# A CIN tower on one core: upper halves of x_pair on ScalarE's queue, alternating PSUM banks, a reordered start

## What is computed

```python
x0 = h = x
for i in range(3):                       # W0: 128 x (32*32), W1 and W2: 128 x (32*64)
    z = (x0[:, :, None, :] * h[:, None, :, :]).reshape(B, F * G, E)
    y = relu(einsum('oc,bce->boe', Ws[i], z) + bs[i][None, :, None])
    if i != n_layers - 1:
        x_keep, h = y[:, :half, :], y[:, half:, :]     # 64 channels are kept, 64 go on
    else:
        x_keep, h = y, y
    xs.append(x_keep)
z = sum(concatenate(xs, axis=1), axis=2)
h = concatenate([z, dense_ctx], axis=1)
h = maximum(h @ W_top1 + b_top1, 0)      # 272 -> 512
h = maximum(h @ W_top2 + b_top2, 0)      # 512 -> 256
y = h @ W_top3                           # 256 -> 1
```

## Time and profile before

| What | Value |
|---|---|
| median of 3 runs | 572.45 us (571.4 to 572.52) |
| the profiled execution: time, span in the profile | 572.41 us, 570.4 us |
| TensorE matmul busy | 526.1 us, 92% |
| VectorE, ScalarE, GpSimd busy | 359.9 us, 135.6 us, 191.6 us |
| direct matmuls (line 559) | 1024 instructions, 451.3 us busy, 31.2 us idle before them |
| DMA over the span | 94.46 MB, mean 166 GB/s |
| mean granted clock of TensorE | 0.976 of full speed |

### The profile page before, as it was taken

The page is one execution under the profiler, slowest core; times in us unless marked ns, Lnnn a source line. Parts: engine busy times, 40 slices in busy tenths (PEclk is TensorE's granted clock), DMA queues, the critical chain, the costliest instruction groups (busy, mean ns, idle before and its releaser), DMA issues.

```text
span 570.4 us, 3875 instructions
## 1 busy us (share of the span) xinstructions
PE 526.1 (92%) x1362; PEld 255.9 (45%) x1362; DVE 359.9 (63%) x212; ACT 135.6 (24%) x193; POOL 191.6 (34%) x162
## 2 busy tenths in 40 slices
PE   2986079699999999999999999999999999999998
PEld 2632034345454544445454545454544445454445
DVE  1243157393949586776949393939495876857642
ACT  1111014312314041414131222213040414130313
POOL 5770072635160707061524334251703030300000
PEclk9988769989999999999999999999999999999999
DMA  6799898279697969697969797796968595540100
GB/s 220 144 187 212 194 263 177 57 201 200 154 230 155 224 146 226 143 230 151 229 141 227 152 239 162 188 214 148 225 149 228 135 236 132 131 94 9 71 0 1
DMA packets 33588, 94.46 MB, mean 166 GB/s; under 512 B 7889, under 2 KB 15057, under 8 KB 25122
## 3 DMA queue, kind: packets, MB, share of 16 engines
q1 hardware_dynamic: 26402, 91.47, 67.3%
q0 software_dynamic: 4096, 1.06, 1.6%
q10 hardware_dynamic: 3072, 1.70, 1.4%
HBM read 92.04 MB, written 2.10 MB: 165 GB/s over the span
## 4 chain that ended last, share of the span: by engine, by line
PE 84%; DMA 8%; POOL 3%; DVE 2%; ACT 1%; issue 1%; ACTq 1%; SPq 0%; DVEq 0%
PE acc L559 74%; PE acc L570 7%; DMA x_rot<-x_scratch 4%; POOL gathered L313 3%; DMA x_scratch<-gathered 2%; DMA gathered<-in_table,rows_all 2%; PE acc L580 1%; DVE z L378 1%; PE acc L575 1%; ACT h L472 0%; DMA row<-in_row 0%; DVE z L366 0%; ACTq L259 0%; PE h L580 0%; ACT kept L472 0%
## 5 line engine op out<-in xcount | busy, mean ns | idle before, releaser
L559 PE MATMUL acc<-z,w_direct 128*128 128x512 f32 x1024 | 451.3, 601 | 31.2 <-DVE z L378 25.7
L559 PEld LDWEIGHTS acc<-z,w_direct 128*128 128x128 f32 x1024 | 196.5, 193 | 276.6 <-issue 243.3
L378 DVE TENSOR_TENSOR z<-h,x_pair 128x2048 f32<-128x2048 f32 (+1 forms) x65 | 144.9, 2250 | 141.3 <-ACT h L472 135.2
L326 POOL TENSOR_TENSOR z_low<-z,z_high 128x1024 fp32r<-128x1024 f32 x30 | 70.2, 2361 | 260.8 <-ACT z_high L458 260.8
L313 POOL DMA_INDIRECT gathered<-in_table,rows_all x128 | 121.1, 946 | 40.7 <-issue 36.0
L378 DVE TENSOR_TENSOR z<-h_odd,x_pair 128x2048 f32<-128x2048 f32 x32 | 72.2, 2279 | 8.8 <-ACT h_odd L472 8.8
L378 DVE TENSOR_TENSOR z<-h_even,x_pair 128x2048 f32<-128x2048 f32 x32 | 72.2, 2279 | 5.2 <-ACT h_even L472 5.2
L472 ACT ACTIVATE h<-acc,columns 64x512 f32<-64x512 f32 x32 | 20.8, 652 | 221.0 <-PE acc L570 215.5
L458 ACT ACTIVATE z_high<-z 128x1024 fp32r<-128x1024 f32 x30 | 30.1, 1049 | 72.4 <-DVE z L366 72.4
L472 ACT ACTIVATE kept<-acc,columns 64x512 f32<-64x512 f32 (+1 forms) x48 | 32.8, 683 | 54.6 <-PE acc L559 53.8
L366 DVE TENSOR_TENSOR z<-x_rep,x_rot 128x2048 f32<-128x2048 f32 x15 | 34.2, 2280 | 16.6 <-DMA x_rot<-x_scratch 16.6
(11 more groups left out here) (119 smaller groups left out, 116.4 us busy)
## 6 DMA issues: line engine op xcount, KB each, us to landing
x_pair<-x_scratch SPq DMA_DIRECT2D x128, 512.0 KB, 6.8
x_rot<-x_scratch SPq DMA_DIRECT2D x56, 256.0 KB, 5.2
x_rep<-x_scratch SPq DMA_DIRECT2D x14, 256.0 KB, 5.0
w_direct<-in_W SPq DMA_DIRECT2D x2, 1024.0 KB, 8.9
gathered<-in_table,rows_all POOLq DMA_INDIRECT x128, 7.1
x_scratch<-gathered SPq DMA_DIRECT2D x30, 64.0 KB, 9.3
x_rot<-x_scratch ACTq DMA_DIRECT2D x4, 256.0 KB, 18.2
x_pair<-in_W_top SPq DMA_DIRECT2D x2, 512.0 KB, 4.3
```

Source lines behind the costliest of these rows:

```text
L326: nc.gpsimd.tensor_tensor(z_low[:, slot_of(pair)], products_of(pair), z_high[:, slot_of(pair)].bitcast(F32), ALU.subtract).then_inc(low_po ...
L378: nc.vector.tensor_tensor(z[:, step.group % Z_SLOTS, first:end], h[:].unsqueeze(1).to_broadcast([P, end - first, N]), x_pair[:, chunk % 2, ...
L559: op = nc.tensor.matmul(acc[pair.layer][:], w_direct[:, first + i], products_of(pair)[:, i], start=i == 0 and pair is OPENS[pair.layer, pa ...
```

## The change

Five things are edited.

1. `load_pair` is split into `load_half`. SyncE's queue issues the lower halves (a = 0) of every chunk, ScalarE's queue the upper halves (a = 1). For chunk 0 and chunk 1 they stand as blocks of four near the head of ScalarE's program, each behind a wait for that chunk's `x_stored`; from chunk 2 on one stands behind each layer-2 step, with a wait for that step's products.
2. `store_x(1)` and `load_x0(1)` go from ScalarE's to SyncE's program, behind chunk 0's lower halves and ahead of chunk 1's.
3. Layers 1 and 2 alternate between two PSUM banks: layer 1 between `spare` (even chunks) and `acc[1]`, layer 2 between `x_bank` and `acc[2]`. `open_bank` waits for the chunk before the last.
4. The places of `layer_out` in ScalarE's program are a table `OUTPUTS`: layer 1 comes ahead of the next chunk's layer 0, layer 2 one step earlier. In `FIRST` the step (0, 2, 0) stands two places earlier in TensorE's order of products, behind (1, 1, 0).
5. The dense input is transposed ahead of TensorE's first transposes (`BUSY` is 56, was 64), and rounded on ScalarE and VectorE there; before, it stood inside chunk 1.

The diff, cut to what matters:

```diff
-BUSY = 64
+BUSY = 56
...
 FIRST = ([(1, 0, k) for k in range(GROUPS)] + [(2, 0, 0), (0, 1, 0)] + [(2, 0, k) for k in range(1, GROUPS)]
-         + [(1, 1, 0), (1, 1, 1), (0, 2, 0), (1, 1, 2), (1, 1, 3)])
+         + [(1, 1, 0), (0, 2, 0)] + [(1, 1, k) for k in range(1, GROUPS)])
...
+def outputs():
+
+    at = {(0, c): PLACE[1, c, 0] for c in range(CHUNKS)}
+    at |= {(1, c): PLACE[2, c - 1, GROUPS - 1] if c >= 2 else PLACE[2, c, 0] for c in range(CHUNKS)}
+    at |= {(2, c): PLACE[2, c + 1, 0] if c else PLACE[1, 1, 1] for c in range(CHUNKS - 1)}
+    return at
...
+        banks = [[acc[0], acc[0]], [spare, acc[1]], [x_bank, acc[2]]]
...
+        def load_half(eng, c, k, a):
+            rows = x_dram[c, ROT * a + GROUP * k:ROT * a + GROUP * (k + 1), :]
+            eng.dma_start(x_pair[HALF * a:HALF * (a + 1), c % 2, GROUP * k:GROUP * (k + 1), :],
+                          rows.unsqueeze(0).to_broadcast([HALF, GROUP, N])).then_inc(xp_here[c % 2][k], 16)
...
             store_x(sp, 0)
-            for c in range(2):
-                for k in range(GROUPS):
-                    load_pair(c, k)
+            sp.wait_ge(x_stored[0], 32)
+            for k in range(GROUPS):
+                load_half(sp, 0, k, 0)
+            store_x(sp, 1)
+            sp.wait_ge(start_done, 1)
+            load_x0(sp, 1)
+            for k in range(GROUPS):
+                load_half(sp, 1, k, 0)
...
-                    load_pair(step.chunk + 2, step.k)
+                    sp.wait_ge(x_stored[step.chunk % 2], 32 * ((step.chunk + 2) // 2 + 1))
+                    load_half(sp, step.chunk + 2, step.k, 0)
...
+            act.wait_ge(x_stored[0], 32)
+            for k in range(GROUPS):
+                load_half(act, 0, k, 1)
             act.wait_ge(small_here, 16 * SMALL)
             act.wait_ge(spread, 1)
             nc.scalar.activation(x_rep[:], rep_bank[:], ACT.Copy).then_inc(first_copied, 1)
             squares(0)
+            act.wait_ge(x_stored[1], 32)
+            for k in range(GROUPS):
+                load_half(act, 1, k, 1)
             for n, step in enumerate(PLAN):
-                if step.layer and step.k == 0:
-                    layer_out(step.layer - 1, step.chunk)
-                    if step is STEPS[1, 0, 0]:
-                        store_x(act, 1)
-                        load_x0(act, 1)
-                for chunk in range(CHUNKS):
-                    if n == PLACE[2, chunk, GROUPS - 1] + RELU2:
-                        layer_out(2, chunk)
+                for layer, chunk in OUTPUTS:
+                    if OUTPUTS[layer, chunk] == n:
+                        layer_out(layer, chunk)
                 if step.layer == 0:
                     squares(step.chunk)
...
+                if step.layer == 2 and step.chunk + 2 < CHUNKS:
+                    wait_made(act, step)
+                    act.wait_ge(x_stored[step.chunk % 2], 32 * ((step.chunk + 2) // 2 + 1))
+                    load_half(act, step.chunk + 2, step.k, 1)
...
-                if pair is OPENS[pair.layer, pair.chunk] and pair.chunk:
-                    pe.wait_ge(kept_out[pair.layer], pair.chunk)
+                used = pair.chunk if pair.layer == 0 else pair.chunk - 1
+                if pair is OPENS[pair.layer, pair.chunk] and used > 0:
+                    pe.wait_ge(kept_out[pair.layer], used)
...
             pe.wait_ge(w_ready, 2)
+            turn_dense()
             for _ in range(BUSY):
                 nc.tensor.transpose(acc[0][:, 0:P], ident[:], ident[:])
...
-                if step is STEPS[1, 1, 0]:
-                    turn_dense()
```

More of the change, by code:

```diff
@@ L97 @@
 PLACE = {(step.layer, step.chunk, step.k): n for n, step in enumerate(PLAN)}
-RELU2, SUM01, SUM2 = 3, 1, 4
+SUM01, SUM2 = 1, 4
+def outputs():
[3 more added lines that the diff above has]
+    return at
+OUTPUTS = outputs()
 def behind():
@@ L244, in wait_made, with bank_of @@
             eng.wait_ge(z_made, step.group)
+        def bank_of(pair):
+            return banks[pair.layer][pair.chunk % 2]
+        def load_half(eng, c, k, a):
+            rows = x_dram[c, ROT * a + GROUP * k:ROT * a + GROUP * (k + 1), :]
+            eng.dma_start(x_pair[HALF * a:HALF * (a + 1), c % 2, GROUP * k:GROUP * (k + 1), :],
+                          rows.unsqueeze(0).to_broadcast([HALF, GROUP, N])).then_inc(xp_here[c % 2][k], 16)
         def store_x(eng, c):
@@ L270, in _ @@
                     w12_here[layer], 16)
[L272 to L277, removed]
             sp.wait_ge(gather_done[0], 16 * GATHERS)
@@ L396, in sum_components @@
                                         kept.rearrange("p (b e) -> p b e", b=ROWS), AX.X, ALU.add).then_inc(made, 1)
+            dve.wait_ge(dense_rounded, 1)
+            nc.vector.scalar_tensor_tensor(
+                out=dense_parts[:], in0=dense_high[:].bitcast(F32), scalar=signs[0:COPIES * EMBED, 2:3],
+                in1=dense_bank[0:COPIES * EMBED, :], op0=ALU.mult, op1=ALU.add).then_inc(dense_ready, 1)
             dve.wait_ge(first_copied, 1)
@@ L416, in _ @@
                         sum_components(chunk, kept2[:], sum2, kept_out[2], sum2_made)
[L417 to L421, removed]
             def split_top(rounded, count, full, high, low, done):
@@ L468, in squares, with relu @@
                 nc.scalar.activation(zl_high[:], zl_full[:], ACT.Copy).then_inc(last_high, 1)
-            def relu(dst, layer, half=None):
+            def relu(dst, bank, layer, half=None):
                 rows = slice(None) if half is None else slice(HALF * half, HALF * (half + 1))
-                return nc.scalar.activation(dst, acc[layer][rows, :], ACT.Relu, bias=bias[rows, layer:layer + 1])
+                return nc.scalar.activation(dst, bank[rows, :], ACT.Relu, bias=bias[rows, layer:layer + 1])
             def layer_out(layer, chunk):
+                bank = banks[layer][chunk % 2]
                 closes = CLOSES[layer, chunk]
@@ L484, in layer_out @@
                         act.wait_ge(sum2_made, chunk)
-                    relu(kept2[:], 2).then_inc(kept_out[2], 1)
+                    relu(kept2[:], bank, 2).then_inc(kept_out[2], 1)
                     return
@@ L494, in layer_out @@
                 h = h1 if layer == 0 else h2[chunk % 2]
-                relu(h[0:HALF, :], layer, 1)
-                relu(h[HALF:P, :], layer, 1).then_inc(h_ready[layer], 1)
-                relu(kept01[HALF * layer:HALF * (layer + 1), chunk % 2], layer, 0).then_inc(kept_out[layer], 1)
+                relu(h[0:HALF, :], bank, layer, 1)
+                relu(h[HALF:P, :], bank, layer, 1).then_inc(h_ready[layer], 1)
+                relu(kept01[HALF * layer:HALF * (layer + 1), chunk % 2], bank, layer, 0).then_inc(kept_out[layer], 1)
             act.wait_ge(sym_made, 1)
@@ L558, in unsplit @@
                 for i in range(2):
-                    op = nc.tensor.matmul(acc[pair.layer][:], w_direct[:, first + i], products_of(pair)[:, i],
+                    op = nc.tensor.matmul(bank_of(pair)[:], w_direct[:, first + i], products_of(pair)[:, i],
                                           start=i == 0 and pair is OPENS[pair.layer, pair.chunk],
```

6 lines of the change are left out of this document (2 added, 4 removed).

## The result

The changed kernel takes 565.78 us (median of 4 runs, 564.11 to 567.27), the kernel before 571.92 us in the same comparison (570.82 to 572.52): 0.9894 of it, 95% interval 0.9854 to 0.9934. The forecast was 562.3 us, its range 557.5 to 568. The profiled execution took 567.13 us (span 565.0); the four runs lie in two pairs, 564.11 and 564.43, 567.13 and 567.27, and experiment 1 shows a likely reason.

What follows compares the result with a forecast made beforehand. TensorE, busy 92% of the span, bounds the kernel; only its waits, chiefly DMA waits at the start, can be won. 9.3 us by (1,2,0) plus 0.8 at the end, 10.1 off 572.41, gave 562.3 us, range 557.5 to 568.

Steps and rivals of the forecast that it cites:

- rival A: Start: two queues carry no more than one, G at 43.4 to 45.4, time 564.4 us; chance 0.20.
- B: Start: the gate, or chunk 2's store ahead of ScalarE's squares, comes later still, at 46 to 51; 566 to 571 us; chance 0.12.
- G: Start: moment chunk 1's store has landed, which ScalarE awaits before its first relu; between 39.3 and 45.4, taken as 42.3.
- the part behind (1,1,0): From (1,1,0) on TensorE: (1,2,0) comes 9.3 us ahead in all, 4.15 of them won before (1,1,0).
- at the end: Last matmuls: layer 2's bank is free for chunk 15, so the 0.70 us relu leaves the path; 0.8 us with hand-overs.
- the head: Head: dense transposes and fewer warm-up transposes cost nothing, since the gate gives 16 us of cover.
- no loss so far: Start: ScalarE's wait for chunk 2's store, until about 67.6, costs nothing, since products of (2,0,0) are made only at 67.5.
- start 70.9 instead of 72.51, 1.6 earlier: Start: products of (2,0,1) begin 3.47 us after those of (0,1,0), at 70.9 instead of 72.51.
- 4.15 us: Gain ahead of (1,1,0): 1.6 from the earlier (2,0,1) and 2.55 of low clock saved; (1,1,0) at 87.25.
- the whole start now hangs on G: Start: h1 of chunk 0 comes some 15 us later behind chunk 1's store, and all that follows waits on it.
- each us of G moves it by one: Total time: every us of G shifts the 562.3 us by one us, giving 559.3 to 565.4.
- Two queues at chunk 0: Chunk 0's `x_pair`, 4.50 MB: through at 38.6 at 226 GB/s or 42.7 at 188 GB/s.

Runs made afterwards that it cites:

- experiment 1: The changed kernel run again unaltered, beside the kernel before on the first chip: 567.16 us, ratio 0.9897.
- experiment 7: The kernel of experiment 3 with one PSUM bank for each layer, on the second chip: 578.04 us, ratio 0.9815 to the kernel before.
- 8: The kernel of experiment 3 with `FIRST` as before the change, (0,2,0) behind (1,1,1), on the second chip: 578.05 us, ratio 0.9814 to the kernel before.
- experiment 3: The changed kernel with the upper halves of chunks 2 to 15 on SyncE's queue, first chip: 561.88 us, ratio 0.9803 to the kernel before.
- experiment 4: The changed kernel with ScalarE's wait for chunk 1's store and chunk 1's upper halves behind the first relu: 566.5 us, ratio 0.9888 to the kernel before.
- experiment 12: The kernel of experiment 3 without the gate and with all halves of chunks 0 and 1 on SyncE's queue, third chip: 575.25 us, ratio 0.9753.
- experiment 2: The changed kernel with chunk 2's first upper half issued behind the squares of (0,1,0): 567.11 us, ratio 0.9892 to the kernel before.
- experiment 10: The kernel of experiment 3 run again unaltered, on the third chip: 572.66 us, ratio 0.9725 to the kernel before.

## Why the prediction was right, and which step was not

The time fell into the range, by the range's width: 10.1 us were forecast and 6.1 measured between the medians, and the range reached up to 568 us because it took in rival A and the first half of B. Rival A's 564.4 us is nearer to the measured 565.78 than the forecast is, but its mechanism, a late G of 44.4, didn't happen.

**Right: the part behind (1,1,0).** The prediction had 9.3 - 4.15 = 5.15 us there and 0.8 at the end, 5.95 together; measured 5.7. Its pieces, from the profiled executions: (1,1,0) to (1,2,0) takes 110.83 - 91.74 = 19.09 us, where before it took 22.01, 2.9 won of 3.5 forecast: the pause ahead of (1,1,1) is 1.36 us where 1.5 was said, but (1,1,1), the way to (1,1,3), and (1,2,0) each come 0.1 to 0.3 later than their offsets. The low clock of 1.72 us is gone, as forecast: eight matmuls take 3.67 us. The wait of `kept` ahead of the last matmuls is gone, worth 1.0 us where 0.8 was said: besides the wait, the 32 matmuls behind it take 13.73 us where they took 14.00. That adds up to the 5.7. The parts overlap: undone one at a time they cost 2.7 (banks, experiment 7) and 4.7 us (order, 8), where undoing all costs 5.7.

**Right: where the gate stands, and the head.** The gate G came at 41.37 (forecast 42.3); the first matmul at 46.65, released by ScalarE's relu 2.5 us behind the gate (forecast 47.5). The wait on `x_rot` ahead of (0,1,0) is gone. The head cost nothing. The middle shows no wait.

**Wrong: "no loss so far".** The step that failed is that ScalarE's wait for chunk 2's store at about 67.6 costs nothing. It ended at 69.67, 2.1 us later, and the squares stood behind it in ScalarE's program. The step "start 70.9 instead of 72.51, 1.6 earlier" became 72.91, 0.4 later, and with it TensorE paused for 3.85 us and lost the 2.55 us of clock again: **4.15 us** of forecast gain were -0.3. In the faster of the executions, where the store came 1.3 us earlier, 3.5 of them were there. Rival B named this place ("chunk 2's store, for which ScalarE now waits ahead of its squares, is late") and had it at 566 to 571 us with 0.12; the measured 565.78 lies at its edge. I had taken the two queues' drain, 67.3, for the store's landing, without spread, though on the next us hung a clock that falls. The drain came as forecast (205 GB/s from 60 to 66 us, 63 from 67 to 68, 12 from there to 69.7); the store landed some 2 us behind it. The trace of the kernel before had a row for this, the issues from 44 to 69 us with KB each and median us to landing:

```profile
x_scratch<-gathered SPq DMA_DIRECT2D x2, 64.0 KB, 20.5
```

There chunk 2's store, issued at 48.29 behind the same bytes, was followed by the first load that needs it at 69.38, 26.1 us behind chunk 1's landing at 43.3. Behind the forecast's G of 42.3 that gives 68.4, an estimate, and not 67.3. Experiment 3 shows the step's own sum without that wait: (1,1,0) at 86.81 against 87.25, and 561.88 us against 562.3.

**Wrong too: "the whole start now hangs on G", "each us of G moves it by one".** The start hangs on the later of two things, G and chunk 2's store. In experiment 4 the first direct matmul came at 33.68 instead of 46.65 and the time stayed. In experiment 1 the first direct matmul came 1.45 us earlier than in the changed kernel's first profile, but the 32 took 17.01 us instead of 15.49, and (2,0,0) came at 66.10, where it had come at 66.02.

**Two queues at chunk 0.** The forecast put them between 188 and 226 GB/s. VectorE had its last tile at 40.8 instead of 42.68 (experiment 4); in the changed kernel the gate hides even this. Rival A's rule from the Trainium skill ("DMA: Bandwidth & Descriptors", "Issuing engines are not separate DMA queues": a second queue saves issue time alone) fits the middle, where it brought nothing; here some 2 us came all the same. They aren't issue time alone: with one queue the last of chunk 0's loads was issued by 23.8 us, and from 24 to 32 us the DMA engines moved 213 GB/s in the kernel before and 206 in experiment 12, the two profiles with one queue, where the eleven with a second one show 217 to 264. On this point the measurement differs from the rule. Why the rate is higher isn't known.

**Left open.** Whether the kernel of experiment 3 gets faster without the gate (ahead it is the next wait on the path) is not known: both tries ran where the start was late for another reason. The new places of `layer_out` and the move of the dense transposes were not undone by themselves, so their share of the 5.7 us isn't known.

## What to carry to other kernels

A DMA that an engine issues with a wait ahead of it makes everything behind it in that engine's program wait too: before loads are moved to a compute engine's queue, list what stands behind each wait and what the landing's spread does to it. A second queue for the same loads brought nothing here where the bytes were hidden anyway, and where they were not, it had chunk 0's loads there some 2 us sooner, but in experiment 2 the small urgent load (`x_rot`) came 2.9 us late beside the big ones; one queue from chunk 2 on, in the right order, gave 561.9 us against 566 to 567. To find where a change acts, measure from one late, common instruction to the end: 473.2 to 473.3 us in nine profiles sorted out at once what no median could.

## What the hardware showed that I had not expected

**A pause can cost as much again.** After 3.85 us of idleness, and eight matmuls in 5.37 us before it, TensorE's next sixteen took 9.69 us; after 1.38 us, and eight matmuls in 6.50 us before it, 7.13 (experiment 1). The 2.5 us of longer pause brought 2.6 us of low clock with them; which of the two differences decided it wasn't tested.

**A slow start on two chips.** On the second and third chips TensorE's matmuls of the head came singly, with gaps that the profile puts down to issue, until about 49 us; the part behind (1,1,0) took the same 473.2 us as on the first chip, so what differs is the start. The chain of experiment 10:

```profile
34.88 1.01 PE acc L606
35.89 2.48 issue
38.37 1.01 PE acc L606
39.38 1.10 issue
40.48 1.01 PE acc L606
41.48 1.79 issue
43.27 1.00 PE h_even L606
```

The cause was not tested. There the kernel before took 16 us more (588.76 against 572.78) and experiment 3's 11 (572.66 against 561.88), so a ratio of one chip is not that of another.
